# Depthwise conv, GELU, pointwise maps and rolled differences on one core: the image load one tile later, the group statistics in pieces between taps, and another order of work on ScalarE, VectorE and GpSimd

## The reference

```
g = _gn(x)                                   # group norm over 8 channels x 56 x 56
h = gelu(depthwise3x3(g, dw_weight))
maps = einsum('bchw,oc->bohw', h, pw_weight) + pw_bias     # 8 maps of C channels
for i, (dx, dy) in enumerate(OFFSETS8):
    out += maps[:, i] * (roll(g, (dy, dx)) - g)
return x + out
```

## Time and profile before

| | before |
|---|---|
| median of 3 runs | 2495.54 us (2495.15 to 2496.66) |
| the profiled execution, its own time | 2494.25 us |
| its span, first to last instruction | 2492.4 us |
| busy: PE, PEld | 2264.2 us (91%), 2043.2 us (82%) |
| busy: DVE, ACT, POOL | 2209.4 us (89%), 1843.0 us (74%), 2031.6 us (82%) |
| mean granted TensorE clock | 0.969 |

### The profile page before, as it was taken

How to read it: one execution, slowest core, us unless ns; L and a number is a source line. 1 busy time by engine, 2 the same in 40 slices (tenths; PEclk the granted TensorE clock), 3 DMA queues, 4 the chain that set the end, 5 groups by cost and what they waited for, 6 DMA issues and landing times.

```text
span 2492.4 us, 34442 instructions
## 1 busy us (share of the span) xinstructions
PE 2264.2 (91%) x10752; PEld 2043.2 (82%) x10752; DVE 2209.4 (89%) x2380; ACT 1843.0 (74%) x2700; POOL 2031.6 (82%) x844
## 2 busy tenths in 40 slices
PE   2999888998889988899988998889988899998998
PEld 2888777988778887788877888788887888888887
DVE  7999979999799997999879999799997999999994
ACT  5868768787577876778667796677966778687774
POOL 4888778887788887888778888778877788887887
PEclk9999999999999999999999999999999999999999
DMA  4003030030300303003030120302103021030000
GB/s 137 23 16 74 23 76 23 23 75 16 75 23 23 75 23 68 23 24 73 23 68 23 38 59 23 74 17 53 44 23 75 16 67 38 16 75 23 23 23 30
DMA packets 45851, 107.36 MB, mean 43 GB/s; under 512 B 2768, under 2 KB 31440, under 8 KB 45392
## 3 DMA queue, kind: packets, MB, share of 16 engines
q1 hardware_dynamic: 45648, 104.88, 15.6%
HBM read 53.49 MB, written 51.38 MB: 42 GB/s over the span
## 4 chain that ended last, share of the span: by engine, by line
issue 33%; DVE 30%; PE 20%; ACT 15%; DVEq 1%; ACTq 1%; POOL 0%; DMA 0%; POOLq 0%; SPq 0%
PE psum L765 20%; DVE psum L664 13%; ACT psum L508 8%; DVE acc L632 4%; DVE psum L610 4%; ACT hid L493 4%; DVE products L610 3%; ACT squares_out L400 1%; DVE moments L570 1%; DVE psum L655 1%; ACT squares_out L390 1%; DVE moments L568 1%; DVE acc L610 1%; ACT psum L479 0%; ACT psum L483 0%
## 5 line engine op out<-in xcount | busy, mean ns | idle before, releaser
L508 ACT ACTIVATE psum<-psum,bias,rstd 128x448 f32<-128x448 f32 x1792 | 1205.8, 694 | 599.9 <-PE psum L765 553.8
L765 PE MATMUL psum<-hhi,w_hi 128*128 128x448 f32 x3584 | 1347.1, 376 | 216.8 <-DVE acc L632 137.2
L765 PE MATMUL psum<-hhi,w_lo 128*128 128x448 f32 x3584 | 1324.1, 369 | 0.0
L333 POOL TENSOR_TENSOR acc<-acc,products 128x1792 f32<-128x1792 f32 x224 | 910.3, 4064 | 304.1 <-DVE products L610 303.8
L765 PE MATMUL psum<-hlo,w_hi 128*128 128x448 f32 x3584 | 1026.6, 368 | 0.3 <-POOL hlo L300 0.3
L765 PEld LDWEIGHTS psum<-hhi,w_hi 128*128 128x128 f32 x3584 | 687.2, 192 | 335.6 <-DVE acc L632 197.4
L664 DVE SCALAR_TENSOR_TENSOR psum<-xn,dw_f,psum 128x896 f32<-128x896 f32 x768 | 881.4, 1148 | 7.7 <-ACT psum L483 0.4
L765 PEld LDWEIGHTS psum<-hhi,w_lo 128*128 128x128 f32 x3584 | 688.1, 192 | 49.0
L765 PEld LDWEIGHTS psum<-hlo,w_hi 128*128 128x128 f32 x3584 | 684.6, 191 | 53.2 <-POOL hlo L300 0.9
L610 DVE TENSOR_TENSOR products<-psum,fields 128x896 f32<-128x896 f32 x448 | 484.6, 1082 | 13.2 <-ACT psum L508 13.0
L610 DVE TENSOR_TENSOR acc<-psum,fields 128x896 f32<-128x896 f32 x224 | 243.4, 1086 | 219.4 <-ACT psum L508 219.4
(11 more groups left out here) (58 smaller groups left out, 543.2 us busy)
## 6 DMA issues: line engine op xcount, KB each, us to landing
out<-outb SPq DMA_DIRECT2D x112, 448.0 KB, 2.6
xpad<-x SPq DMA_DIRECT2D x30, 1568.0 KB, 15.0
fields<-x SPq DMA_DIRECT2D x4, 784.0 KB, 6.7
xpad<-pw_t SPq DMA_DIRECT2D x1, 2048.0 KB, 12.0
dw_f<-dw SPq DMA_DIRECT2D x1, 9.0 KB, 8.0
pb_f<-pw_b SPq DMA_DIRECT2D x1, 8.0 KB, 7.8
```

The lines of the kernel that those rows point to most:

```text
L333: nc.gpsimd.tensor_tensor(a, a, products[:, k - 2].rearrange("p g s x -> p (g s x)"), ALU.add).then_inc(added_s, 1)
L508: nc.scalar.activation(m, m, ACT.Identity, bias=bias[ip][:, g, d:d + 1], scale=rstd[ip][:, g:g + 1]).then_inc(biased_s, 1)
L765: last = nc.tensor.matmul(maps(q)[:, side, :], w[:, kk, col:col + P], h_part(h, t, nl, kk), start=s == 0, stop=s == len(steps) - 1)
```

## The change

- SP: the load of the next image is issued in tile 0, in front of that tile's output, in place of tile 6 behind `add_x`. It no longer has a wait of its own; the output of tile 6, in front of it in SP's list, waits for that tile's `fold`.
- Statistics: `minus_mean` on ACT writes its accumulator straight into `moments` and a new ACT step `variance` does so with the mean of squares. Four DVE instructions go (`reduce_sum` of `part_sq`, the two scalings into `moments`, and `neg_mean`; POOL's `shift` now reads the negated mean). The other ten are given out in pairs at five places of tile 3, behind the first tap after product 4.
- ACT: `gelu` after unit 0, `start_conv` after unit 1, the cast after unit 2, `normalise` after unit 7. The sums have 12 steps, in tiles 1, 2 and 3.
- DVE: the taps' order at the end of a tile is product 4, tap, product 5, tap, product 6, tap, tap, product 7, tap.
- POOL: `differences`, `split_h`, `add_x`, `norm_scales`, the two `add_pair`, `fold`.

```
-        GELU_AT, HHI_AT, NORM_AT = 0, 1, 5
+        GELU_AT, START_AT, HHI_AT, NORM_AT = 0, 1, 2, 7
-        MEASURE_AT = ((0, 5), (0, 7), (1, 2), (1, 4), (1, 6), (1, 7), (2, 2), (2, 4), (2, 6), (2, 7))
-        STATS_AT = (3, 1)
+        MEASURE_AT = ((1, 2), (1, 4), (1, 5), (1, 6), (2, 2), (2, 3), (2, 4), (2, 6), (2, 7), (3, 2), (3, 3), (3, 4))
+        STATS_TILE = 3
...
-                    if t == TILES - 1 and not last:
-                        sp.wait_ge(xadd_s, n0 + (nl + 1))
-                        load_image(b0 + par + 2, par)
+                    if t == 0 and not (last and nl):
+                        load_image(b0 + par + 1, 1 - par)
...
+                    if more(1):
+                        differences(b0, nl + 1)
                     if more(2):
                         split_h(n0, nl + 2)
-                    if t == 3 and not (last and par):
+                    add_x(n0, nl)
+                    if t == STATS_TILE and not (last and par):
                         norm_scales(b0 + par + 1, 1 - par)
-                    if more(1):
-                        differences(b0, nl + 1)
-                    add_x(n0, nl)
...
+            def variance(g):
+                nc.scalar.activation(part_var[:, g, :], part_sq[:, g, :], ACT.Copy, scale=1.0 / (H * W),
+                                     accum_out=moments[:, 2 * g + 1:2 * g + 2]).then_inc(measure, 1)
...
-                        if u == GELU_AT and more(3):
+                        if u == START_AT and more(3):
                             start_conv(n0, b0, nl + 3)
...
                 dve.wait_ge(measure, b * MEASURES + MEASURES)
-                then(nc.vector.reduce_sum(sums[:, 0:HALVES], part_sq[:], axis=AX.X))
-                then(nc.vector.tensor_scalar(moments[:, 0:3:2], neg_mean_c[:], -1.0, None, ALU.mult))
-                wait()
-                then(nc.vector.tensor_scalar(moments[:, 1:4:2], sums[:, 0:HALVES], 1.0 / (H * W), None, ALU.mult))
-                wait()
                 then(nc.vector.transpose(mom_t[:], moments[:]))
+                yield
                 wait()
                 then(nc.vector.reduce_sum(sums[:], by8(mom_t[:]), axis=AX.X))
+                yield
...
+                    def stats_next():
+                        for _step in itertools.islice(stats, 2):
+                            pass
...
-                    if (t, 1) == STATS_AT and not (last and par):
-                        group_stats(b0 + par + 1)
...
                     kept_product(n0, nl, 4)
                     tap_next()
+                    stats_next()
+                    kept_product(n0, nl, 5)
+                    stats_next()
                     tap_next()
-                    kept_product(n0, nl, 5)
+                    stats_next()
+                    kept_product(n0, nl, 6)
+                    stats_next()
                     tap_next()
-                    kept_product(n0, nl, 6)
-                    tap_next()
+                    stats_next()
                     tap_next()
                     kept_product(n0, nl, 7)
+                    tap_next()
```

More of the change, by code:

```diff
@@ L201, in preact_directional_conv @@
         PROD0, ADD0, FOLD0, SENT0 = UNITS, ADDS, 2, 16
[L202 to L203 removed]
+        HALF_STEPS = 2 * SLICES + 2
+        MEASURES = HALVES * HALF_STEPS
+        STAT = 10
         SCALES = 3
         CONSTS = 5
[L206 removed]
         FIRST = SLICES + 2 + 2 * (SLICES - 1)
@@ L290, in norm_scales @@
                 pool.wait_ge(scales, j * SCALES + 1)
-                nc.gpsimd.tensor_tensor(shift[par][:], neg_mean[:], rstd[par][:], ALU.mult).then_inc(scales, 1)
+                nc.gpsimd.tensor_tensor(shift[par][:], mean_b[:, 0:3:2], rstd[par][:], ALU.mult).then_inc(scales, 1)
                 nc.gpsimd.tensor_tensor(bias[par][:], pb_f[:], window(rstd[par][:], [[1, HALVES], [0, DIRS]]),
@@ L395, in minus_mean @@
                 nc.scalar.activation(part_neg[:, g, :], part_sums[:, g, :], ACT.Copy, scale=-1.0 / (H * W),
-                                     accum_out=neg_mean_c[:, g:g + 1]).then_inc(measure, 1)
+                                     accum_out=moments[:, 2 * g:2 * g + 1]).then_inc(measure, 1)
             def slice_squares(rows, g, c):
-                nc.scalar.activation(squares_out[:], rows, ACT.Square, bias=neg_mean_c[:, g:g + 1],
+                nc.scalar.activation(squares_out[:], rows, ACT.Square, bias=moments[:, 2 * g:2 * g + 1],
                                      accum_out=part_sq[:, g, c:c + 1]).then_inc(measure, 1)
+            def variance(g):
+                nc.scalar.activation(part_var[:, g, :], part_sq[:, g, :], ACT.Copy, scale=1.0 / (H * W),
+                                     accum_out=moments[:, 2 * g + 1:2 * g + 2]).then_inc(measure, 1)
             def measure_step(b, par, i):
@@ L432, in measure_first @@
                         minus_mean(0)
+                    elif i <= 2 * SLICES:
+                        slice_squares(first[:, 0, i - SLICES - 1], 0, i - SLICES - 1)
                     else:
-                        slice_squares(first[:, 0, i - SLICES - 1], 0, i - SLICES - 1)
+                        variance(0)
                 for c in range(SLICES):
@@ L441, in measure_first @@
                 slice_squares(first[:, 1, SLICES - 1], 1, SLICES - 1)
-                act.sem_inc(measure, MEASURES - HALF_STEPS - 1)
+                act.wait_ge(first_s, FIRST)
+                act.wait_ge(measure, HALF_STEPS + 1)
+                variance(1)
+                act.sem_inc(measure, MEASURES - HALF_STEPS - 2)
             def normalise(b0, c):
@@ L591, in group_stats @@
                                                     ALU.add, ALU.add))
-                then(nc.vector.tensor_scalar(neg_mean[:], mean_b[:, 0:3:2], -1.0, None, ALU.mult))
+                yield
             def product(n0, nl, u, to):
@@ L678, in measure_first @@
                 dve.wait_ge(first_s, SLICES + 1)
-                nc.vector.tensor_scalar(neg_mean_c[:, 1:2], sums[:, 0:1], -1.0 / (H * W), None,
+                nc.vector.tensor_scalar(moments[:, 2:3], sums[:, 0:1], -1.0 / (H * W), None,
                                         ALU.mult).then_inc(first_s, 1)
@@ L683, in measure_first @@
                     nc.vector.tensor_scalar(centered, first[:, 1, c].rearrange("p r w -> p (r w)"),
-                                            neg_mean_c[:, 1:2], None, ALU.add).then_inc(first_s, 1)
+                                            moments[:, 2:3], None, ALU.add).then_inc(first_s, 1)
                     dve.wait_ge(first_s, SLICES + 3 + 2 * c)
@@ L697, in _ @@
             dve.wait_ge(first_s, FIRST)
-            dve.wait_ge(consts, CONSTS)
-            group_stats(0)
+            for _step in group_stats(0):
+                pass
             dve.wait_ge(weights_in, 16)
@@ L722, in tap_next @@
                             tap(n0, b0, nl + 3, j)
+                    stats = iter(group_stats(b0 + par + 1) if t == STATS_TILE and not (last and par) else ())
+                    def stats_next():
+                        for _step in itertools.islice(stats, 2):
+                            pass
                     first_product(n0, nl, 0)
```

18 lines of the change are left out of this document (13 added, 5 removed).

## The result

| | before | after |
|---|---|---|
| median of 4 runs on the same chip | 2495.82 us | 2371.36 us (2370.67 to 2373.96) |
| ratio, 95% interval | | 0.9503 [0.9487, 0.952] |
| the profiled execution, its span | 2494.25, 2492.4 us | 2372.03, 2370.2 us |
| busy: PE, DVE | 91%, 89% | 93%, 91% |
| busy: ACT, POOL | 74%, 82% | 77%, 86% |

2385 was predicted. L numbers are those of the changed kernel from here on: L622 products, L676 and L667 taps, L518 `add_bias`, L503 `gelu`, L493 `start_conv`, L474 `normalise`, L576 to L602 the statistics, L285 to L289 `norm_scales`, L230 the loop, L238 the image load.

The account below looks back on a forecast made before the run. Bound: the ring of last tap, `gelu`, `start_conv`, scaling, product 1 and DVE. 2494.25 less 56 (statistics and plain tiles), 54 (branch) and 0.3 gave 2384, median 2385; own range 2366 to 2401, 8 in 10 2362 to 2440.

Parts of the forecast that it names:

- Plain tile: Ordinary tiles, product 1 to product 1: 19.98 us against 20.09, 0.11 gained a tile.
- the sentence that taking the centre tap out of the chain is no gain: Plain tile: `start_conv` leaving the chain gains nothing alone, since product 7 no longer stands behind the last tap as cover.
- Tiles 1 and 2: Measuring step and cast ahead of unit 3's scaling make DVE wait for product 3: 0.6 us lost in each tile.
- Tile 3: Statistics tile: 23.75 us, 3.8 above a plain one, ended by the chain of statistics, POOL, `normalise`, scaling and `gelu`.
- The 7.9 of before: Excess us per image over plain tiles in the kernel before, nearly all in tiles 1 to 3 with the statistics.
- The third rival: Tiles 1 to 3: ACT's lateness is twice that reckoned, or DVE waits again, 1.3 more each: 2443 us; chance 0.11.
- second rival: Tile 3: five small DVE statistics instructions each wait 2.02 us for POOL: 10 us an image, 2535 us; chance 0.04.
- the 7.3 at which it would have decided against the change: Cost in us an image of small instructions waiting for POOL, from 110/15, four of five such instructions.
- The branch: Six taken loop branches, code queued behind the image load: 1.2 us lost in place of 10.2, 54 us gained.
- The first rival: The branch costs 8 to 9 us whatever the DMA queues do, so 54 us are not gained: 2439; chance 0.19.
- The load: Image load issued in tile 0 lands just before the first sum; its rival, landing late, 2400 us, chance 0.03.
- The low end of its own range: 2366 us: 2385 less 6 and 13, for free fetch, statistics at 1.5 and no wait at product 2.

Follow-up runs that it names:

- The square: Four kernels, last tap ahead of or behind product 7, `start_conv` right behind `gelu` or after unit 1: plain tiles 20.09, 20.96, 19.1 to 19.8, and 19.98 (changed kernel).
- e7: Changed kernel with POOL's `norm_scales` moved behind the first `add_pair`, so POOL works while the statistics run: 2429.25 us.
- e2: Changed kernel with the image load put back into tile 6 behind `add_x`: 2437.32 us.
- e5: Kernel before with the image load moved into the next tile and the sums' first steps moved out of tile 0: 2441.6 us.
- e1: Kernel before with the image load alone moved into the next tile, tile 0: 2530.76 us.
- e4: Changed kernel with the old order of taps alone (product 7 behind the last tap), ACT's order as changed: 2349.3 us.
- e10: Changed kernel with the old order of taps and the ten statistics in one row at their first place in tile 3: 2334.87 us.

## Why the prediction was right, step by step

By the profiled execution 110 us were predicted (2494.25 to 2384) and 122.2 came (2494.25 to 2372.03). Each step's mechanism came as written; the 12 us more are mostly two costs, of tile 3 and of the branch, taken a little too large.

- **Plain tile**: 19.98 predicted and measured. Last tap at 16.64 of the tile (16.54 predicted), product 0 at 17.70 (17.59), `gelu` to product 1 2.16 (2.16), product 2 at 2.17 with a wait of 0.1 (2.17). The square confirms the sentence that taking the centre tap out of the chain is no gain as long as DVE's cover shrinks with it.
- **Tiles 1 and 2**: 0.51 and 0.60 over a plain tile; 0.6 each predicted.
- **Tile 3**: right in mechanism, the term mis-sized. 3.8 over a plain tile predicted, 3.32 measured: the statistics end at 17.4 (17.8), because the ten take 1.66 and not 1.9 and the squares hold products 2 and 3 by 0.07 and 0.39, not 0.2 and 0.5. From there the chain went as written: POOL 1.15, `normalise` at 18.7, `gelu` at 21.2 (21.6), product 1 at 23.30 (23.75). With tiles 1 and 2 this gives 4.3 an image in place of 3.7, so 64 us against 56. (The working has a slip of 0.1 here: 19.05 and twice 1.22 make 21.5 for `gelu`, not 21.6.) The 7.9 of before holds the fall of PE's clock shown above; the forecast took it as measured and built the new tile from its own terms, with PE never the bound, which held (granted clock 1.00), so that the gap did it no harm. The third rival (ACT's lateness twice as large) did not come.
- **The small instructions behind POOL** (second rival): not paid, for the reason that was given (POOL's list stands at `norm_scales`); e7 shows what it costs otherwise, 3.86 an image for one instruction. That is below the 7.3 at which it would have decided against the change.
- **The branch**: 1.2 predicted, 0.95 measured, from 10.4 (10.2 by `fold`): 57 us against 54. ACT's fetch takes 2.7 in place of the 3.3 that I took from PE, `gelu` is at 18.7 (18.9), product 1 at 20.8 (21.1), and product 2 has no second spell, as forecast. PE's clock stayed at 1.00 there, as forecast. The first rival is shown wrong by e2 and e5.
- **The load**: no wait for it in the sums; its landing is unchanged at 10.5 to 18.7 us. e1 shows what it costs where they are too early.
- What is left, about 1 us, is the last images' tiles and the pass that falls through the branch.

The working had one more gap: it took the load's move as separate from the sums' table, which e1 shows it is not. In this change both moved, so the sum did not suffer. The low end of its own range was also added up short: by its terms (fetch for nothing 6 us, statistics at 1.5 another 15 x 0.4 = 6, no wait at product 2 some 105 x 0.1 = 10) it is about 2362 and not 2366. The measured 2371 lies inside both.

## What to carry to other kernels

When a transfer is moved, find its first reader and move the two together; and keep the queues empty where a loop branches back, since the next code comes by the same engines. Taking an instruction out of a chain pays only if the engine that waits for the chain keeps work to do meanwhile: try each half of a reordering by itself, as the faster kernel here had one of the two. Before a small instruction that costs a microsecond is removed, look at what the neighbour engine does at that moment. And when a row of small instructions holds up a product, look at PE's granted clock behind it: it may have fallen, and then the matmuls behind the pause cost time too.

## What the runs showed of the hardware

- **Code behind a taken branch**: with DMA queues free of the load ACT goes on 2.5 to 2.7 us after its branch and DVE 2.8 to 3.1, over the six branches of the changed kernel, by the sequencer's rows; under the image load ACT needed 8.3 to 9.1 and DVE 7.7 to 8.4 before (branch of ACT at 1271.2, next at 1280.26). PE's branch itself is recorded with 3.3 to 3.8 in both.
- **How long code waits behind the load**: 353 packets took 102.1% of 16 engines for 6 us, so 0.278 us each. The Trainium skill, "DMA: Bandwidth & Descriptors", section "Queues, rings and completion order", gives a packet 9 to 17 descriptors, 64 at most. If what the profile counts are those descriptors, an estimate by that page for one turn is 2.5 to 4.7 us, and the wait of 6 us would be one to two turns. The page then would not speak against the stall, which the prediction took it to do unless the packets are long. No run here tells this apart.
- **Matmuls at two paces with the same granted clock**: the two windows of e4 both have PE fully busy and a clock of 1.00, and 96 matmuls take 19.84 or 19.31, about 207 and 201 ns each. It is not the DMA traffic: two further tiles of e4 take 19.84 with a DMA share of 0.06 (from 302.80) and 19.34 with 0.70 (from 485.90). What chooses the pace stays open; where PE is the bound it is worth 0.5 us a tile.
- **A pause of 2 us on PE** was followed by a stretch of 3.6 us at a mean granted clock of 0.54 to 0.64 in seven images and by none in the other eight of the same kernel (e10); the long images are 0.85 us longer. Behind pauses of 5.8 to 6.3 us, in tile 3 of the kernel before, the clock fell in all 15 images (mean 0.57 to 0.85 over the 6 us from 12 us behind product 1).
